# Setup loads on two queues, stack rows set during the loads, and the rotation table loaded behind a half stack

## Time and profile before

| | |
|---|---|
| Median of three runs | 3108.23 us (3107.77 to 3111.34) |
| The profiled execution's own time | 3121.12 us |
| Its span in the trace | 3119.4 us |
| PE busy | 2755.0 us, 88% |
| PE weight load busy | 1747.3 us, 56% |
| DVE busy | 1894.0 us, 61% |
| ACT busy | 1213.2 us, 39% |
| POOL busy | 743.2 us, 24% |
| DMA | 193.99 MB, 25.0% of 16 engines |
| Granted PE clock, mean | 0.917 of full speed |

### The profile page before, as it was taken

One profiled execution on the slowest core, in us unless ns is written; L12 is line 12 of the kernel. 1 busy time (PEld: TensorE's weight loads), 2 busy tenths in 40 slices (PEclk: granted clock), 3 DMA queues, 4 the chain that ended last, 5 costly groups with the idle time before them and its releaser, 6 DMA issues.

```text
span 3119.4 us, 45976 instructions
## 1 busy us (share of the span) xinstructions
PE 2755.0 (88%) x15374; PEld 1747.3 (56%) x15374; DVE 1894.0 (61%) x5539; ACT 1213.2 (39%) x2706; POOL 743.2 (24%) x1274
## 2 busy tenths in 40 slices
PE   2885899989998998989989998989998999989987
PEld 2563566456655566466655566555664666554544
DVE  6443666665567566665666665675667666666642
ACT  0321243444344343434434443344434344344451
POOL 1321132223222231222322232222322133121110
PEclk8986899999999999999999999999999999999996
DMA  2014103411333113412044113331134212343211
GB/s 56 1 41 124 28 16 67 119 39 31 59 86 93 45 31 63 124 45 57 20 102 119 34 31 66 86 93 43 33 70 124 53 42 34 83 113 88 54 29 42
DMA packets 137424, 193.99 MB, mean 62 GB/s; under 512 B 49439, under 2 KB 111214, under 8 KB 127854
## 3 DMA queue, kind: packets, MB, share of 16 engines
q1 hardware_dynamic: 137198, 191.07, 25.0%
HBM read 122.34 MB, written 67.63 MB: 61 GB/s over the span
## 4 chain that ended last, share of the span: by engine, by line
PE 63%; DVE 13%; DMA 9%; issue 3%; ACT 2%; POOL 2%; SPq 1%; DVEq 0%; ACTq 0%; POOLq 0%
PE bank L728 9%; PE bank L761 7%; PE bank L742 7%; DMA stk<-k_halves 7%; PE bank L564 4%; PE bank L657 4%; PE bank L504 3%; PE bank L544 3%; PE bank L671 3%; PE bank L513 3%; PE bank L495 2%; DVE bank L1080 2%; PE bank L658 2%; PE bank L599 2%; PE bank L681 2%
## 5 line engine op out<-in xcount | busy, mean ns | idle before, releaser
L1283 ACT ACTIVATE pexp<-bank 128x512 f32<-128x512 f32 (+3 forms) x1536 | 675.0, 495 | 604.4 <-PE bank L742 602.6
L728 PE MATMUL bank<-stk,stq 128*128 128x512 f32 (+3 forms) x1536 | 629.9, 424 | 146.2 <-DMA stk<-k_halves 50.0
L1080 DVE CUSTOM_DVE_ANT_0 bank<-bank,maskneg 128x128 f32<-128x128 f32 (+3 forms) x1024 | 501.1, 497 | 418.1 <-PE bank L728 412.0
L728 PEld LDWEIGHTS bank<-stk,stq 128*128 128x128 f32 x1536 | 305.3, 201 | 527.8 <-issue 453.1
L742 PE MATMUL bank<-stq,stk 128*128 128x512 f32 (+3 forms) x1536 | 533.8, 420 | 56.2 <-ACT pexp L1283 52.6
L1083 DVE TENSOR_REDUCE mxa<-bank 128x1 f32<-128x512 f32 x512 | 351.8, 687 | 156.8 <-PE bank L728 151.3
L1431 POOL TENSOR_SCALAR_AFFINE_SELECT pexp<-pexp 128x256 f32<-128x256 f32 x512 | 213.4, 423 | 777.5 <-ACT pexp L1283 777.3
L742 PEld LDWEIGHTS bank<-stq,stk 128*128 128x128 f32 x1536 | 278.9, 200 | 197.2 <-ACT pexp L1283 122.3
L761 PE MATMUL bank<-pexp,vsm 128*32 128x512 f32 (+3 forms) x3072 | 357.0, 539 | 8.8 <-POOL pexp L1431 8.6
L1349 POOL TENSOR_SCALAR_AFFINE_SELECT arena<-arena 128x512 f32<-128x512 f32 x128 | 79.1, 642 | 415.8 <-ACT arena L1187 415.8
L564 PE MATMUL bank<-arena 32*128 32x256 f32 x1024 | 157.1, 426 | 15.3 <-DVE arena L888 11.2
(11 more groups left out here) (183 smaller groups left out, 4192.5 us busy)
## 6 DMA issues: line engine op xcount, KB each, us to landing
stq<-q_halves SPq DMA_DIRECT2D x128, 256.0 KB
arena<-rope_table SPq DMA_DIRECT2D x8, 2048.0 KB
q_halves<-arena SPq DMA_DIRECT2D x32, 512.0 KB, 3.0
k_halves<-arena SPq DMA_DIRECT2D x32, 512.0 KB, 2.8
stk<-k_halves SPq DMA_DIRECT2D x64, 256.0 KB
stk<-k_halves SPq DMA_DIRECT2D x128, 128.0 KB
v_rows<-arena SPq DMA_DIRECT2D x16, 544.0 KB, 4.2
vsm<-v_rows SPq DMA_DIRECT2D x16, 544.0 KB, 3.8
```

Source lines behind the costliest of these rows:

```text
L728: mm(bk[:, 0:k1 - k0], stq[b_][:, h % 2, qb * P:(qb + 1) * P], stk[b_][:, h % 2, k0:k1], start=True, stop=True).then_inc(s["r_full"], 1)
L1080: nc.vector.tensor_tensor_reduce(out=sc, in0=sc, in1=maskneg[:, CH - (k1 - k0):CH], scale=1.0, scalar=LOWEST, op0=ALU.add, op1=ALU.max, ac ...
L1283: nc.scalar.activation(pexp[:, u % NPX, j, 0:n], ps(j)[:, 0:n], ACT.Exp, scale=DK ** -0.5).then_inc(s["exp_done"], 1)
```

## The change

In the setup block SP issues only the ten large loads and x, and no longer waits for w_mem. ACT issues the 27 small ones, after the wait for w_mem, ahead of its one instruction in the block. DVE clears only the five stk buffers, then waits until that is done and writes the rows of ones, all ahead of its wait for the loads; nothing of it is left at its end. POOL clears the five stq buffers, one after the other with a wait after each, behind its masks and ahead of its wait for DVE. In front_sp the rotation table's DMA is issued four ticks later, at 120 b + 74, and so behind the stack load of that tick for b of 1 and more; the steps after it stay at their ticks.

```diff
 @block.sync
-    sp.wait_ge(w_mem, 2)
     for i, w in enumerate((a["L0_ffn_W_r"], ... a["L1_attn_Wo"])):
         load(raw[:, i], w.rearrange("(k p) c -> p k c", p=P))
     load(wqkv[:], ...)
     load(wo0[:], ...)
-    load(rawp[0:PROJ], a["L1_ffn_Wp"])
-    ... (26 more small loads)
     for c in range(NC):
         sp.dma_start(x[:, 4 * c:4 * c + 4], ...).then_inc(w_x[c], 16)

 @block.gpsimd
     select(hmask[:], ALU.is_ge, 0.0, DK - 1, [[DK, H // KT]], -1).then_inc(w_pool, 1)
+    pool.wait_ge(w_pool, 10)
+    for i, st in enumerate(stq):
+        nc.gpsimd.memset(st[MROW:P].bitcast(F32), 0.0).then_inc(w_zeroq, 1)
+        pool.wait_ge(w_zeroq, i + 1)
     pool.wait_ge(w_dve, 4)

 @block.scalar
+    act.wait_ge(w_mem, 2)
+    load(rawp[0:PROJ], a["L1_ffn_Wp"])
+    ... (26 more small loads, act.dma_start)
     act.wait_ge(w_dve, 2)

 @block.vector
-    for st in (*stq, *stk):
+    for st in stk:
         nc.vector.memset(st[MROW:P].bitcast(F32), 0.0).then_inc(w_zero, 1)
+    dve.wait_ge(w_zero, NSLOT)
+    for st in stk:
+        nc.vector.memset(st[MROW:SROWS].bitcast(F32), 1.0)
     dve.wait_ge(w_in, 16 * NLOAD)
     ...
-    dve.wait_ge(w_zero, 2 * NSLOT)
-    for st in stk:
-        nc.vector.memset(st[MROW:SROWS].bitcast(F32), 1.0)

 def front_sp(c, b):
     yield from idle(52)
     if c == 0:
-        yield from idle(14)
+        yield from idle(18)
         for p in range(2):
             f_gone(sp, 1, b, "lo", p)
         sp.dma_start(ropet[:]..., rope_d...)
-        yield from idle(11)
+        yield from idle(7)
```

More of the change, by code:

```diff
@@ L171, in macaron @@
         w_x = [sem("w_x0"), sem("w_x1")]
-        w_zero = sem("w_zero")
+        w_zero, w_zeroq = sem("w_zero"), sem("w_zeroq")
         w_tr, w_cp, w_dve, w_act, w_ps2 = sem("w_tr"), sem("w_cp"), sem("w_dve"), sem("w_act"), sem("w_ps2")
@@ L187, in _ @@
             def _(sp):
-                n = 0
                 def load(dst, src):
-                    nonlocal n
                     sp.dma_start(dst, src).then_inc(w_in, 16)
-                    n += 1
-                sp.wait_ge(w_mem, 2)
                 for i, w in enumerate((a["L0_ffn_W_r"], a["L0_ffn_W_k"], a["L0_ffn_W_v"], a["L1_attn_Wq"], a["L1_attn_Wk"],
@@ L280, in _, with load @@
             def _(act):
+                n = 10
+                def load(dst, src):
+                    nonlocal n
+                    act.dma_start(dst, src).then_inc(w_in, 16)
+                    n += 1
+                act.wait_ge(w_mem, 2)
+                load(rawp[0:PROJ], a["L1_ffn_Wp"])
+                r0 = 0
+                for e, r in enumerate(RANKS):
+                    load(rawd[r0:r0 + r], a[f"L1_ffn_Wd{e}"])
+                    for j in range(4):
+                        load(rawu[:, :, j, r0:r0 + r], a[f"L1_ffn_Wu{e}"].rearrange("(k p) r -> p k r", p=P))
+                    r0 += r
+                for m, w in enumerate((a["L0_ffn_mu_k"], a["L0_ffn_mu_r"])):
+                    load(mu[:, m, 0, :], w.rearrange("(k p) -> p k", p=P))
+                load(bpb[:], a["L1_ffn_bp"].partition_broadcast(P))
+                load(rsim[0:PROJ, 0], a["L1_ffn_sim"])
+                load(rsim[0:PROJ, 1, 0:1], a["L1_ffn_temp"].partition_broadcast(PROJ))
+                load(rsim[0:PROJ, 2, 0:1], a["L1_ffn_bp"].rearrange("(p o) -> p o", o=1))
+                assert n == NLOAD, n
                 act.wait_ge(w_dve, 2)
```

## The result

The changed kernel takes 3076.9 us at the median of six runs (3059.91 to 3081.79), the kernel before 3109.78 beside it (3101.9 to 3123.34): the ratio is 0.9886, 95% interval [0.9857, 0.9915]. In six more runs (experiment 1) it is 3076.43 us and 0.9891 [0.9862, 0.9919]. So it gained 33 to 34 us of the 49.6 forecast. The profiled execution was the fastest of its runs, 3059.91 us, 61 us less than the profiled one of before; that pair alone would have confirmed the forecast with room to spare, wrongly.

The account below looks back on a forecast made before the run. PE's list was taken to set the time, transfers counting where PE waits, plus the setup. Setup 14.3, stalls 22.0 and clock 13.3 make 49.6 us, off 3108.2: 3059 (3048 to 3068 at 0.66; range 3046 to 3082).

Parts of the forecast that it names:

- The seven waits: PE's score products at L728 wait for a stack behind the table, b = 1 to 7; all go, 22.0 us.
- the rival of a late table: The table lands later than 513, DVE waits ahead of L796, half of 35.3 us is given back: 3076, chance 0.2.
- Setup: Before the main block: earlier fills and loads start it at about 34.1 instead of 48.43, saving 14.3 us, bounds 10.7 to 14.3.
- The tail of five fills: At the end of DVE's setup: five fills of 2.14 us, 10.7 us in all, go whatever the loads do.
- POOL and DVE: In the setup: POOL's five fills take 1.9 us each, run beside DVE's without slowing them, and cost nothing.
- lock: Rival in the setup: fills on POOL and DVE hold each other up; chance 0.05.
- Stalls: PE's seven stack waits of 2.51 to 4.78 us vanish when the stack is issued ahead of the table: 22.0 us.
- a cushion: DVE stands 3.69 us for PE behind L796, so a small miss by the table is covered.
- Half of the engines: The table's DMA keeps half of the DMA engines for 20 us, and half of the stack stands behind it.
- Clock term: PE's clock stays up behind the seven removed stack waits: 13.3 us, 78% of 17.0.
- upper bound of 17.0: All half-speed time in the ten us behind each of the seven waits is regained: 17.0 us.
- the bound 0: Nothing is regained from the clock, because another gap of PE brings it down instead: 0 us.

Follow-up runs that it names:

- experiment 1: The changed kernel timed again with no edit, against the kernel before: 3076.4 us, ratio 0.9891.
- experiment 4: The kernel before with only the fills moved as in the change, all 37 loads staying on SP: 3103.7 us, ratio 0.9986.
- experiment 8: The changed kernel with small loads dealt in turn to ACT and SP and the fills of ones on POOL: 3070.8 us, 0.9869 of the kernel before.
- Experiment 2: The kernel before with only the rotation table's load four ticks later, old setup: 3078.1 us, ratio 0.9906.
- experiment 7: The changed kernel with the rotation table's load another four ticks later: 3155.9 us, 1.0155 of the kernel before.
- experiment 6: The new setup with the table at its old tick, issued as eight one-row DMAs instead of one: 3073.5 us, 0.9889 of the kernel before.
- 9: The changed kernel with three spare products on PE ahead of its next gap, a 1.65 us wait for ACT: 3061.7 us, 0.9849 of the kernel before.
- 5: The kernel before with six spare products on PE ahead of each of the seven stack waits: 3088.1 us, ratio 0.9939.
- 3: The changed kernel with the table's load back at its old tick, so only the setup changed: 3091.5 us, 0.9951 of the kernel before.

## Why the prediction was right or wrong

The measured 3076.9 lies inside the range of 3046 to 3082, but outside the 3048 to 3068 that had the chance of 0.66. The gain was two thirds of the forecast. The seven waits, the fills and the order of the loads came out by their mechanism; one term of the sum did not come at all. That the rival of a late table names 3076 is chance: no DVE wait for the table is in the trace of the kernel after.

**Setup, forecast 14.3, measured 12.2 in this pair, 11.3 on average.** The tail of five fills went as worked out, 10 to 10.8 in experiment 4. The loads landed at 21.57, not by 19.2 to 21, and at 22.0 to 23.0 in five other executions: ACT took (19.83 - 1.37) / 27 = 0.68 us for an issue, where SP had taken 0.55, the price that was borrowed. PE then began only 0.9 us ahead of DVE instead of 3, and the copies still came 0.85 us apart.

**POOL and DVE.** As forecast: five fills beside DVE's on POOL at (9.23 / 5) 1.85 us, and DVE's still every 2.14. Five fills of POOL in experiment 8, for half of their time beside an idle DVE, took 9.22 us, no less. That fills on the two engines hold each other up ("lock", chance 0.05) is shown by no run.

**Stalls, forecast 22.0.** All seven went, in every kernel with the table behind the stack. Experiment 2's span times clock fell by 26.5, the 22 and some 4 not accounted for. The table came in time: its data ended near 497, issued at 472.95, 3 us before DVE asked at 499.99. The rival of a late table was far from coming, but experiment 7 shows how little cover there was for it: the 3.69 us that DVE stood for PE covered half a us of 11.66. The forecast counted that idle time as a cushion, but PE's scores wait for maxima that are queued behind DVE's wait.

**Half of the engines.** The old order's harm needed the table's one DMA ahead of the stack; spread wider (6) it does none. That it kept half of them to itself was the author's estimate from its share of 0.49; the trace doesn't show which engines carried it. That at twice the share it would also be twice as fast, as experiment 6 expected, is wrong.

**Clock term, forecast 13.3, measured 4 +- 4, most of which is the setup's (experiment 1). This is the step that failed.** Its upper bound of 17.0 is from the ten us behind each of the seven waits of the kernel before, with a mean clock of 0.66 to 0.67 three times and of 0.83 four times, two of them in the earlier trace rows. It said that the clock, up ahead of the wait, would stay up without it. It did: 17.1 us of loss became 0. What it left out is the next gap. It was listed as the bound 0 ("another gap brings the clock down instead"), and the value was then taken at 78% of the other bound. The gap of 1.65 us for ACT had been there before, cost 15.4 us, and costs 32.4 now at the same length; filling it gave 15 us (9). That the loss behind it doubled is shown: over the seven sequences it is 27.3 to 32.4 us in the six profiled kernels in which PE doesn't stand for the stack and the gap is as it was (after, experiments 1, 2, 5, 6 and 8), and 15.4 to 17.1 in the three with the stack wait (before, 3 and 4). Why it did isn't shown. It isn't that any stall ahead keeps it short: behind the 11 us stalls of experiment 7 it is 23.9 us.

With 12.2 + 22.0 = 34.2 and nothing for the clock the forecast would have been 3074; measured, 3076.9 and 3076.4.

## What to carry to other kernels

Before a large broadcast or table load is put on a queue, see which small load behind it is needed first, and let that one go ahead; then check what else stands in that queue at the new place. Count a removed stall at its length, and count the clock behind it only after looking for the next gap of PE, and fill both with spare products if they can't be removed. Where runs of one kernel differ by 20 us through the clock, one profiled execution proves nothing about 30: compare span times mean clock and the loss to the clock over many runs, and read small edits from several traces. Remember that a stall at the low clock counts as loss too, 27 us of it in experiment 7.

## What the runs showed of the hardware that was not expected

- Low stretches behind one and the same gap of 1.65 us cost 1.7 to 5.1 us each, and how many are long (over 3 us) changes with what PE did some 40 us earlier: one of seven in the kernel before, all seven in the kernel after.
- An idle PE in a wait can cost more than the wait: products that nobody needs, 5.36 us of them in stalls of 2.5 to 4.8, made the kernel 0.6% faster.
- The 27 small loads took 0.68 to 0.74 us an issue on ACT, beside SP's large ones, where SP took 0.54 or 0.55 alone. But dealt out to both (experiment 8) they took 0.64 on ACT and 0.66 on SP, so it isn't shown that the engine makes the difference and not the other queue beside it.
- Eight rows of 16 KB, each written to 16 partitions, ran at 106 GB/s with a share of 0.49 of the engines as one DMA and at 132 GB/s with a share of 1.10 as eight.
